# Zeroing the slot buffer: twelve of 79 fills moved from late attention steps to steps 4 and 8

## The chip, the cores and the metric

The kernel runs on one NeuronCore of a Trainium2 chip. The metric is the device time of one execution in microseconds. The core has five engines that work side by side and meet at semaphores: TensorE (PE, with its weight loads shown apart as PEld), VectorE (DVE), ScalarE (ACT), GpSimd (POOL) and SyncE (SP). SP computes nothing; it issues DMAs in the order of its program and waits for semaphores between them. The DMAs themselves run on the core's 16 DMA engines.

## The reference, cut to what matters

One decoder layer in float32 on one sequence of 2048 tokens of width 512.

```python
x = x + attention(layernorm(x), ...)   # q, k, v: projection, short conv, silu; delta rule with state S; rms norm; Wo
x = x + ffn(layernorm(x), ...)

# ffn
cw = combine_weights(xt, gate_w)       # softmax over 16 experts, 2 of 4 groups, top 4 experts, normalised
for e in range(16):
    out = out + cw[:, e:e+1] * (swiglu(xt @ up[e].T) @ down[e].T)
out = out + swiglu(xt @ shared_up.T) @ shared_down.T
```

In the kernel the 2048 tokens form 16 tiles of 128 rows. For the experts the kernel gathers tokens: each of the 2048 x 4 chosen (token, expert) pairs is written as a row of 532 bytes into `slot_rows` in DRAM, a buffer of NQ = 79 slots of 128 rows (64 full tiles and up to 15 tiles that are only partly filled). A row that nobody writes must be zero, so the whole buffer is zeroed before the rows are scattered into it. What is moved here is the zeroing.

## The kernel before, in words

**The attention** (`attention`, first 565 us) is one hand-written schedule. A step `u` runs from -8 to 18, and each step has six slots `s` = 0 to 5. Every engine has its own copy of the same double loop and issues in slot (u, s) what belongs there; the engines are held together by semaphores alone. Step u works on tile u of the delta rule (the hops through the state S on PE, L1081, L1107 and L1147, L1121, L1126), on the projections of later tiles, and on the norm, gate logits and stores of tiles u-1, u-2 and u-3. One step takes some 28 us in the middle of the attention.

**The inverse.** Per tile a triangular matrix (its gram blocks) must be inverted. Four tiles are inverted together on DVE (`inverse`, parts 0 to 8, first instruction L1484). To lay the blocks of four tiles over the lanes, SP stores the gram blocks of each tile to DRAM (`store_gram`, L401, four DMAs) and loads them back turned (`load_lanes`, L408), which waits until the four stores of that tile have landed. For the tiles 12 to 15 this happens in steps 8 to 10: stores and loads of tile 12 and 13 in step 8, the store of tile 14 in step 9 slot 4, `load_lanes(14)` and `store_gram(15)` in step 9 slot 5, `load_lanes(15)` in step 10 slot 0. DVE starts the inverse of these four in step 10 slot 1. On DVE the row sums of the output (L1464), the copy of the gate logits (`lg`, L1478) and the residual Rs (L1448) of that step stand behind it. The four tiles 8 to 11 do the same in steps 4 to 6.

**Weights and the shared expert.** From step 10 on SP also loads the shared expert's weights: the first part of `shared_up` in step 10, its second part in step 12 slot 0 together with two tiles of partial sums (`sq`), and `shared_down` (L441, L442) with the second group of turned activations (`front_region<-x2n_turned`, L447, four DMAs of 256 KB) in step 13 slot 0. PE fits matmuls of the shared expert between the hops, two to a slot (L1204, L1214 for gate and up of the shared units).

**The zero fills.** `zero_rows` (L454 to L457) issues one DMA on SP that fills the next slot of 128 rows from a small tile of zeros:

```python
            def zero_rows():
                if zeroed[0] < NQ:
                    sp.dma_start(rows[zeroed[0]], zeros[:, :].unsqueeze(1).to_broadcast([P, DC, RW // DC])).then_inc(s_zeroed, 16)
                    zeroed[0] += 1
```

It waits for nothing, and nothing waits for it until the end of the attention (`attention_stored`). It is called at the end of a slot, so it stands on SP's queue behind all that the slot issues. Calls beyond the 79th do nothing. Twelve are issued in the opening slots, the others one to a slot from step 0 on, except where the condition at L564 leaves slots out.

**After the attention** come the routing, the scatter of rows into `slot_rows` (GpSimd), the rest of the shared expert and the loop over the 79 slots with the experts' weights, where PE is bound by its matmuls.

Of the kernel before, what the change touches and what calls it, by code (L numbers as in the profile page):

```python
# [201 lines left out]
def attention(nc, es, x_d, wq_d, wk_d, wv_d, wb_d, cq_d, ck_d, cv_d, nw_d, wo_d, gw_d, shu_d, shd_d, region, wsh,  # L202
# [180 lines left out]
    with nc.Block() as block:  # L383

        @block.sync
        def _(sp):
# [67 lines left out]
# [4 lines that stand above are left out]
# [16 lines left out]
            for u in range(FIRST, LAST):  # L474
                even = u % 2 == 0
                for s in range(SLOTS):
# [85 lines left out]
                    if 19 <= opening(u, s) < 28 or 33 <= opening(u, s) < 36:  # L562
                        zero_rows()
                    if u >= 0 and not (u % 4 == 3 and s >= 2) and not (u % 4 == 1 and s >= 4) and not (u % 4 == 2 and s < 1) \  # L564
                            and not (u == 10 and s >= 2) and not (u == 11 and s < 2):
                        zero_rows()
            assert zeroed[0] == NQ
            for par in range(2):
# [1826 lines left out]
```

How the kernel before makes its waits and increments, by code:

```python
def local_routing(dve, link, linked, lg, z, sc, rank, sel, mx, sm, gs, grank, gsel, tri, pa, pb, s_z, s_e, s_sel, lo, n, part):  # L116
# [21 lines left out]
        link(dve.tensor_tensor(pa[:, 0:m * k * k], pa[:, 0:m * k * k], pb[:, 0:m * k * k], ALU.add))  # L138
        linked()
        link(dve.tensor_reduce(out, pa[:, 0:m * k * k].rearrange("p (t e j) -> p t e j", e=k, j=k), AX.X, ALU.add))
    if part == 0:
        linked()
        link(dve.tensor_reduce(mx[:, at], lg[:, at, :], AX.X, ALU.max))
        linked()
        dve.tensor_tensor(z[:, at, :], lg[:, at, :], over(mx[:, at], E), ALU.subtract).then_inc(s_z, 1)
    if part == 1:
        dve.wait_ge(s_e, done + 1)
        link(dve.tensor_reduce(sm[:, at], z[:, at, :], AX.X, ALU.add))
        linked()
        link(dve.reciprocal(sm[:, at], sm[:, at]))
# [22 lines left out]
        if part % 2 == 0:  # L174
            beats(sc[:, four, :], pa, E, ALU.is_gt)
            beats(sc[:, four, :], pb, E, ALU.is_equal)
            linked()
            ties_of_earlier(TPG, E)
        else:
            count(rank[:, four, :], TPG, E)
    if part == 4 + ranks:
        linked()
        dve.tensor_scalar(sel[:, at, :], rank[:, at, :], float(K), None, ALU.is_lt).then_inc(s_sel, 1)
        dve.wait_ge(s_sel, done + 1)
        link(dve.tensor_tensor(sc[:, at, :], sc[:, at, :], sel[:, at, :], ALU.mult))
        linked()
        link(dve.tensor_reduce(sm[:, at], sc[:, at, :], AX.X, ALU.add))
# [8 lines left out]
def least(eng, sem, n):  # L196
    if n > 0:
        eng.wait_ge(sem, n)
```

## Time and profile before

| | |
|---|---|
| median of 3 runs | 1313.39 us (1312.79 to 1316.36) |
| the profiled execution | 1320.15 us |
| its span in the profile | 1318.4 us |
| mean granted clock of TensorE | 0.987 |
| busy: PE / DVE / ACT / POOL | 97% / 66% / 28% / 26% of the span |
| moved by DMA | 171.09 MB, mean 130 GB/s |

Windows count in microseconds from the span's start. The granted clock is a share of full speed: 1.00 is 2.4 GHz, 0.50 is 1.2 GHz, and a number between them is a stretch that had both. The DMA share is the time of the packets as a share of 16 engines; since packets overlap, it can be over 1 where the engines are full. A DMA row on SPq shows how long SP took to issue, not how long the data travelled; for several DMAs in a row it is the time from the first issue to the end of the last.

### The profile page before, as it was taken

How to read it: one execution, taken by the hardware profiler on the slowest of the kernel's cores; microseconds unless marked ns; L12 is line 12 of the kernel's file. 1: busy time of each engine (PE TensorE's matmuls, PEld its weight loads, DVE VectorE, ACT ScalarE, POOL GpSimd, SP SyncE). 2: the span in 40 equal slices, each digit the busy share in tenths (PEclk: the TensorE clock that was granted, in tenths of full speed). 3: DMA queues.
4: the chain of work that ended last, by engine and by line, in shares of the span. 5: the costliest groups of instructions: out<-in, count | busy, mean ns of one | idle time of the engine just before them, and what ended most of it. 6: DMA issues, size and time to landing. Idle time of an engine off the chain costs nothing.

```text
span 1318.4 us, 27847 instructions
## 1 busy us (share of the span) xinstructions
PE 1275.2 (97%) x8725; PEld 795.6 (60%) x8726; DVE 866.4 (66%) x2411; ACT 373.7 (28%) x818; POOL 340.3 (26%) x398
## 2 busy tenths in 40 slices
PE   7979999999999999999999999999999999999997
PEld 6857777877876555443444555555555555555553
DVE  4897698769779226544111677777777777777774
ACT  4754655654553223220000011111111111111111
POOL 1202225323242222115652021222121212122212
PEclk9989999999997999999999999999999999999999
DMA  5434853752653694575457456666666666564420
GB/s 162 86 54 93 135 118 82 163 119 68 131 120 125 156 205 107 130 236 207 182 212 236 111 131 132 138 133 138 136 138 134 132 134 132 131 138 71 74 50 9
DMA packets 208517, 171.09 MB, mean 130 GB/s; under 512 B 71473, under 2 KB 160561, under 8 KB 208433
## 3 DMA queue, kind: packets, MB, share of 16 engines
q1 hardware_dynamic: 135056, 114.16, 34.0%
q0 software_dynamic: 16496, 34.23, 13.3%
q10 hardware_dynamic: 56880, 21.54, 7.8%
q8 instruction: 57, 0.93, 0.3%
q14 instruction: 28, 0.22, 0.1%
HBM read 91.06 MB, written 82.73 MB: 132 GB/s over the span
## 4 chain that ended last, share of the span: by engine, by line
PE 54%; DVE 2%; issue 0%; DMA 0%; POOL 0%; ACT 0%; DVEq 0%; POOLq 0%
PE pD L2300 15%; PE pG L2275 14%; PE pU L2284 14%; PE pG L2232 3%; PE pU L2232 3%; PE pD L2251 3%; PE pU L2226 1%; PE pD L2246 0%; DVE ups L2173 0%; DMA out<-y,ix 0%; DVE w L1873 0%; DVE w L1874 0%; DVE route_keep L1872 0%; POOL out L2065 0%; DVE qf L1885 0%
## 5 line engine op out<-in xcount | busy, mean ns | idle before, releaser
L2173 DVE STREAM_TRANSPOSE ups<-a 32x96 f32<-32x96 f32 (+1 forms) x1248 | 326.0, 261 | 42.4
L2065 POOL DMA_INDIRECT out<-y,ix x79 | 123.0, 1557 | 479.1 <-ACT y L2126 306.7
L2300 PE MATMUL pD<-w,ups 128*128 (+1 forms) x474 | 216.6, 592 | 0.7 <-DVE ups L2173 0.7
L2284 PE MATMUL pU<-w,xsT 128*128 x632 | 199.9, 459 | 0.0
L2275 PE MATMUL pG<-w,xsT 128*128 x632 | 199.9, 458 | 0.0
L2275 PEld LDWEIGHTS pG<-w,xsT 128*128 128x128 f32 x632 | 119.5, 189 | 88.4 <-issue 37.6
L2284 PEld LDWEIGHTS pU<-w,xsT 128*128 128x128 f32 x632 | 120.1, 190 | 66.9
L974 PE MATMUL pProj<-front_region 128*128 128x256 f32 x624 | 153.7, 389 | 2.2 <-ACT front_region L711 1.6
L2300 PEld LDWEIGHTS pD<-w,ups 128*128 128x128 f32 (+1 forms) x474 | 90.0, 190 | 93.2 <-issue 76.8
L974 PEld LDWEIGHTS pProj<-front_region 128*128 128x128 f32 x624 | 112.6, 190 | 19.8 <-ACT front_region L711 2.0
L2126 ACT ACTIVATE y<-pD,wq 128x512 f32<-128x512 f32 x79 | 54.3, 687 | 246.7 <-PE pD L2300 236.9
L2115 ACT ACTIVATE g<-pG 128x352 f32<-128x352 f32 x79 | 36.7, 464 | 260.2 <-DVE xsT L2161 176.6
L1386 DVE SCALAR_TENSOR_TENSOR front_region<-front_region,cw 128x256 f32<-128x256 f32 x216 | 102.3, 515 | 10.5 <-ACT front_region L747 8.0
L2194 DVE TENSOR_TENSOR a<-g,pU 128x352 f32<-128x352 f32 x79 | 41.2, 521 | 89.1 <-PE pU L2284 81.1
L2050 POOL DMA_INDIRECT slot_rows<-xall,pos x64 | 62.8, 981 | 52.4 <-DMA slot_rows<-xall,pos 47.2
L636 POOL TENSOR_TENSOR TT<-TT,ng 128x512 f32<-128x512 f32 x16 | 17.7, 1106 | 223.7 <-ACT TT L789 137.9
L1448 DVE TENSOR_TENSOR Rs<-pC,vh 64x512 f32<-64x512 f32 x32 | 22.0, 688 | 60.2 <-PE pC L1081 59.9
L1164 PE MATMUL pT<-wo,oT 128*128 128x512 f32 x128 | 59.1, 604 | 0.4 <-ACT oT L816 0.4
L2161 DVE STREAM_TRANSPOSE xsT<-xs 128x512 f32<-128x512 f32 x79 | 55.6, 703 | 5.6 <-DMA xs<-slot_rows 4.9
L2251 PE MATMUL pD<-front_region 128*128 128x512 f32 x120 | 53.1, 597 | 0.0
L746 ACT ACTIVATE front_region<-pProj 128x256 f32<-128x256 f32 x78 | 30.1, 385 | 77.5 <-PE pProj L974 75.3
L2232 PE MATMUL pG<-front_region 128*128 128x512 f32 x112 | 50.4, 593 | 0.6 <-PEq L383 0.6
(258 smaller groups left out, 1651.1 us busy)
## 6 DMA issues: line engine op xcount, KB each, us to landing
w<-in_up_T SPq DMA_DIRECT2D x16, 1408.0 KB
slot_rows<-zeros SPq DMA_DIRECT2D x79, 266.0 KB
xs<-slot_rows ACTq DMA_DIRECT2D x316, 64.0 KB
w<-in_down_T SPq DMA_DIRECT2D x16, 512.0 KB
front_region<-in_L_attn_hidden_states SPq DMA_DIRECT2D x16, 256.0 KB, 3.9
x2r<-in_L_attn_hidden_states SPq DMA_DIRECT2D x16, 256.0 KB, 4.5
partial_sums<-x2r SPq DMA_DIRECT2D x16, 256.0 KB, 3.4
x_normed<-x2n SPq DMA_DIRECT2D x16, 256.0 KB, 2.0
```

Of the source, the lines that this page charges most:

```text
L974: mm = pe.matmul(proj_bank(g), w3[:, w, k, cols(i % DC, P)], xnT[p % 2][:, k, :], start=(k == 0), stop=(k == DC - 1))
L1164: mm = pe.matmul(pT1[:, 0, :], oT[:, k, :], wo[:, k, :], start=(k == 0), stop=(k == DC - 1))
L1386: ins = dve.scalar_tensor_tensor(out=acc[(g + h) % len(acc)], in0=raw[:, at, j:j + PW], scalar=cw[:, at, j:j + 1], in1=acc[(g + h) % len(a ...
L2050: pool.indirect_dma_start(out=xs_d[:, :], out_offset=bass.IndirectOffsetOnAxis(ap=pos[:, i, j:j + 1], axis=0), in_=xall[:, i, :], in_offse ...
L2065: pool.indirect_dma_start(out=flat, out_offset=bass.IndirectOffsetOnAxis(ap=ix[1 - par][:, 0:1], axis=0), in_=y[1 - par][:, :], in_offset= ...
L2161: dve.transpose(xsT[par][:, :, :].rearrange("p k (a i) -> p a k i", a=BLOCKS), xs[par][:, :].rearrange("p (a k j) -> p a k j", a=BLOCKS, k ...
L2173: dve.transpose(aT[par][B * to:B * to + B, 0:n, rows], a[rows, 0:len(IC) * P].rearrange("p (c n) -> p c n", c=len(IC))[:, 0:n, B * to:B * ...
L2232: mm = pe.matmul(p[:, :], wsh["up"][:, k, at:at + P], xg[gr % 2][:, k, :], start=(k == 0), stop=(k == DC - 1))
L2251: mm = pe.matmul(sdown(j)[:, :], sa[:, c, P * i:P * i + P], wsh["down"][:, c, :], start=False, stop=(c == UNITS - 1))
L2275: mm = pe.matmul(pG[0][:, 0:I], xsT[par][:, k, :], w[:, bass.ds(slot, 1), 2 * I * k:2 * I * k + I], start=(k == 0), stop=(k == DC - 1))
L2284: mm = pe.matmul(pU[0][:, 0:I], xsT[par][:, k, :], w[:, bass.ds(slot, 1), 2 * I * k + I:2 * I * (k + 1)], start=(k == 0), stop=(k == DC - 1))
L2300: mm = pe.matmul((pYlast if end(q) else pYq)[:, :], aT[1 - par][0:m, c, :], down[0:m, :, UPW + D * c:UPW + D * (c + 1)], start=(c == 0), s ...
```

## The change

The condition under which a slot of the steps from 0 on issues a zero fill leaves out steps 12 and 13 now, and in steps 4 and 8 every slot issues a second one.

```diff
                     if u >= 0 and not (u % 4 == 3 and s >= 2) and not (u % 4 == 1 and s >= 4) and not (u % 4 == 2 and s < 1) \
-                            and not (u == 10 and s >= 2) and not (u == 11 and s < 2):
+                            and not (u == 10 and s >= 2) and not (u == 11 and s < 2) and u not in (12, 13):
+                        zero_rows()
+                    if u in (4, 8):
                         zero_rows()
```

The fills by step, before and now: step 4: 6 and 12; step 8: 6 and 12; step 12: 6 and 0; step 13: 4 and 0; step 16: 5 and 3 (the count of 79 is reached sooner); all other steps as before.

SP in step 8, before: the stores of tile 12 (L401), its lane load (L408), the stores and the lane load of tile 13, with fills (L456) between.

```order
177 L401 DMA gram_blocks<-NP 32x8x32 x3
178 L456 DMA slot_rows<-zeros 512x1x133 x2
179 L408 DMA front_region<-gram_blocks 32x1024 [waits inverse_done,gram_stored0]
...
184 L456 DMA slot_rows<-zeros 512x1x133
185 L401 DMA gram_blocks<-NP 32x8x32 [waits gram_scaled]
186 L401 DMA gram_blocks<-NP 32x8x32 x3
187 L456 DMA slot_rows<-zeros 512x1x133
188 L408 DMA front_region<-gram_blocks 32x1024 [waits inverse_done,gram_stored1]
189 L456 DMA slot_rows<-zeros 512x1x133
```

The same place of SP's queue now:

```order
177 L401 DMA gram_blocks<-NP 32x8x32 x3
178 L456 DMA slot_rows<-zeros 512x1x133 x4
179 L408 DMA front_region<-gram_blocks 32x1024 [waits inverse_done,gram_stored0]
...
184 L456 DMA slot_rows<-zeros 512x1x133 x2
185 L401 DMA gram_blocks<-NP 32x8x32 [waits gram_scaled]
186 L401 DMA gram_blocks<-NP 32x8x32 x3
187 L456 DMA slot_rows<-zeros 512x1x133 x2
188 L408 DMA front_region<-gram_blocks 32x1024 [waits inverse_done,gram_stored1]
189 L456 DMA slot_rows<-zeros 512x1x133 x2
```

Every fill of the step is doubled, ahead of the next tile's stores and of the loads that wait for them; step 4 has the same picture with tiles 8 and 9.

SP in steps 12 and 13, before, from the second load of partial sums (L452) to the last fill of step 13's first two slots:

```order
242 L452 DMA sq<-partial_sums 128x512 [waits x2_stored1]
243 L456 DMA slot_rows<-zeros 512x1x133 x2
244 L520 DMA x_normed<-x2n 128x512 [waits x2n_ready]
245 L522 DMA x2n_turned<-x2g 128x512 [waits x2nT_ready]
246 L456 DMA slot_rows<-zeros 512x1x133
247 L526 DMA x2r<-in_L_attn_hidden_states 128x512 [waits x2_stored0,x2n_ready]
248 L456 DMA slot_rows<-zeros 512x1x133 x3
249 L488 DMA partial_sums<-x2r 128x512 [waits x2_ready]
250 L441 DMA front_region<-in_shared_down_T 64x512 x2
251 L442 DMA front_region<-in_shared_down_T 128x5x512
253 L447 DMA front_region<-x2n_turned 128x4x128 x3
254 L456 DMA slot_rows<-zeros 512x1x133 x2
```

The same place now:

```order
242 L452 DMA sq<-partial_sums 128x512 [waits x2_stored1]
243 L520 DMA x_normed<-x2n 128x512 [waits x2n_ready]
244 L522 DMA x2n_turned<-x2g 128x512 [waits x2nT_ready]
245 L526 DMA x2r<-in_L_attn_hidden_states 128x512 [waits x2_stored0,x2n_ready]
246 L488 DMA partial_sums<-x2r 128x512 [waits x2_ready]
247 L441 DMA front_region<-in_shared_down_T 64x512 x2
248 L442 DMA front_region<-in_shared_down_T 128x5x512
250 L447 DMA front_region<-x2n_turned 128x4x128 x3
```

No fill stands ahead of or behind the weight loads any more; the order of everything else is as it was. No other engine's order changes.

## Rows read from the trace of the kernel before

**Rows 1.** The page: busy time by engine; instruction queue (packets, MB); the zero fills.

```profile
PE 1275.2 (97%) x8725; PEld 795.6 (60%) x8726; DVE 866.4 (66%) x2411; ACT 373.7 (28%) x818; POOL 340.3 (26%) x398
...
q8 instruction: 57, 0.93, 0.3%
...
slot_rows<-zeros SPq DMA_DIRECT2D x79, 266.0 KB
```

**Rows 2.** Windows: length, busy us of PE, PEld, DVE, ACT, POOL; clock, DMA share, GB/s.

```profile
457.00:464.00 7.00, 7.00 (x117) 4.32 (x113) 2.29 (x5) 2.35 (x5) 2.34 (x6) 1.00 1.15 214
464.00:470.00 6.00, 4.30 (x70) 2.69 (x69) 0.77 (x2) 1.78 (x3) 3.10 (x4) 1.00 1.24 127
470.00:475.00 5.00, 5.00 (x41) 3.02 (x40) 0.00 (x0) 0.98 (x2) 0.00 (x0) 0.66 1.04 200
```

**Rows 3.** Timeline of PE's weight loads, step 13: start, us, instruction, idle before.

```profile
466.66 0.19 PEld L1214 LDWEIGHTS pT<-front_region 128*128 128x128 f32 x1 [0.24 <-issue]
469.37 0.19 PEld L1214 LDWEIGHTS pT<-front_region 128*128 128x128 f32 x1 [2.52 <-issue]
```

**Rows 4.** Timeline of SP's queue, steps 12 and 13.

```profile
458.19 4.39 SPq L456 DMA_DIRECT2D slot_rows<-zeros  x3
...
465.48 0.64 SPq L442 DMA_DIRECT2D front_region<-in_shared_down_T  x1
466.16 10.54 SPq L447 DMA_DIRECT2D front_region<-x2n_turned  x4
```

**Rows 5.** Timeline of SP's queue, steps 9 and 10: gram stores and lane loads.

```profile
376.86 1.94 SPq L401 DMA_DIRECT2D gram_blocks<-NP  x4
382.19 0.31 SPq L408 DMA_DIRECT2D front_region<-gram_blocks  x1
383.38 2.40 SPq L401 DMA_DIRECT2D gram_blocks<-NP  x4
...
386.99 0.31 SPq L408 DMA_DIRECT2D front_region<-gram_blocks  x1
```

**Rows 6.** DMA issues in 386.9 to 387.2 us: KB each, us to landing.

```profile
front_region<-gram_blocks SPq DMA_DIRECT2D x1, 128.0 KB, 2.3
```

**Rows 7.** Timeline of DVE, step 10.

```profile
389.30 0.17 DVE L1484 COPY route_keep<-front_region 128x4 f32<-128x4 f32 x1
...
392.61 0.17 DVE L1478 COPY lg<-pT 128x16 f32<-128x16 f32 x1 [1.16 <-PE pT L1178]
...
396.75 0.69 DVE L1448 TENSOR_TENSOR Rs<-pC,vh 64x512 f32<-64x512 f32 x1
```

**Rows 8.** Timeline of PE, step 10.

```profile
393.80 0.66 PE L936 MATMUL pT<-ident,x2n 128*128 128x128 f32 x4
...
397.59 0.24 PE L1107 MATMUL pC<-Rs,TT 64*64 64x64 f32 x1 [0.16 <-DVE Rs L1448]
```

**Rows 9.** Timelines of SP's queue and of DVE, step 6: the same for tiles 8 to 11.

```profile
275.79 0.34 SPq L408 DMA_DIRECT2D front_region<-gram_blocks  x1
...
284.18 0.17 DVE L1484 COPY route_keep<-front_region 128x4 f32<-128x4 f32 x1
```

**Rows 10.** Windows of steps 8 and 9, and one of dense zero fills (step 0).

```profile
349.00:361.00 12.00, 12.00 (x145) 8.56 (x142) 7.68 (x17) 6.05 (x16) 0.00 (x0) 1.00 1.09 202
361.00:362.50 1.50, 1.50 (x29) 1.22 (x23) 0.04 (x1) 1.50 (x5) 0.00 (x0) 1.00 0.17 21
370.00:374.50 4.50, 4.50 (x93) 3.94 (x91) 3.98 (x10) 3.13 (x7) 4.31 (x3) 1.00 0.18 65
142.00:149.00 7.00, 6.81 (x144) 5.58 (x142) 5.00 (x10) 5.54 (x14) 6.24 (x11) 1.00 1.22 143
```

**Rows 11.** Windows at half clock: in the opening, and in steps 10 and 11.

```profile
95.40:102.20 6.80, 6.42 (x48) 5.15 (x49) 6.70 (x11) 2.55 (x7) 2.52 (x5) 0.50 0.01 2
406.00:419.60 13.60, 12.60 (x148) 8.92 (x143) 13.34 (x19) 3.64 (x7) 6.62 (x9) 0.50 0.19 62
```

## Prediction

> **What bounds the kernel now.** I read the page first. TensorE (PE) is busy 97% of the span [rows 1], so only two things can move the end: a stretch in which PE stands, and a stretch in which its clock is halved. The change moves DMAs alone, so I looked, with the views of windows and of timelines, for places where a DMA stands behind such a stretch. There are two in the attention.
>
> **Place A, step 13, around 468 us.** Between 464 and 470 us PE is busy 4.30 of 6.00 us, while the DMA engines are more than full (share 1.24) and yet move only 127 GB/s; in 457 to 464 they moved 214 [rows 2]. The weight-load timeline shows the hole: in the middle of one tile (pT by L1214, where nothing is waited for) the next load comes 2.52 us late, "issue" being all that the profile can say [rows 3]. Behind it the granted clock is 0.66 in 470 to 475 [rows 2], a mixture of 2.4 and 1.2 GHz. SP's own timeline shows the crowd: three zero blocks take 4.39 us to issue, and the four loads of x2n_turned 10.54 us, against some 0.5 us for one where the queue is free (four in 1.94 us [rows 5]).
>
> **Place B, step 10, 389.3 us.** The last load of the gram lanes (L408, tile 15) is issued at 386.99 [rows 5] and lands 2.3 us later [rows 6], at 389.29. VectorE (DVE) begins the inverse of the last block (L1484), which waits for it, at 389.30 [rows 7]. That load has no slack: by how much it comes later, by so much DVE stands. DVE matters there: it runs nearly without a gap up to Rs at 396.75 [rows 7], and PE waits 0.16 us for that Rs at 397.59 [rows 8].
>
> **The change, part by part.** In the code 79 zero blocks stay 79. Steps 12 and 13 lose six and four, step 16 its last two (all 79 are out before); steps 4 and 8 gain six each. Each is one SP DMA of 266 KB [rows 1], without a wait of its own. Nothing on PE, DVE, ScalarE or GpSimd changes.
>
> *Removed in steps 12 and 13.* The six blocks of step 12 stand ahead of the shared down weights and the x2n_turned loads [rows 4]. What remains in the queue moves in long rows and finds its place before 466 us. I take it that the hole goes, since it fell in the stretch of lowest rate: 6.00 - 4.30 = 1.70 us of PE, and the clock's share, (1 - 0.66) x 5 = 1.7 us, together **-3.4 us**. Bounds: 0 if something else made the hole; -4.2 if all 2.52 us of the late weight load counts beside the clock. PE is busy all of 457 to 464 and of 470 to 475 [rows 2], so what is won there is not lost to another wait.
>
> By the Trainium skill ("Runtime: NRT & Kernel Launch", Instruction fetch mechanics) an engine's instructions come in 16 KiB blocks by a DMA queue, mostly hidden. The instruction queue of the page has 57 packets with 0.93 MB [rows 1], 16 KB each, which agrees. By that rule the hole is a block of instructions that came late through full DMA engines; the sum would be the same -3.4.
>
> *Added in step 4.* One block more in each slot. The next inverse starts at 284.18 behind other DVE work, while its last lane load is issued at 275.79 [rows 9]; with 2.3 us to land, as in [rows 6], that leaves 6.1 us. There are free stretches too. I count 0 here; if that cover is gone, the price is that of place B.
>
> *Added in step 8.* One block costs the DMA engines 1.9 us where they carry zero blocks back to back (272 KB at 143 GB/s, 142 to 149 us) and 1.35 us at the mixed rate of step 8 (202 GB/s) [rows 10]. The share is already 1.09 in 349 to 361, so six more are a queue of 6 x 1.9 = 11.4 us, or 8.1. What is free after it is 0.83 x 1.5 us at 361 and 0.82 x 4.5 us at 370 [rows 10], together 4.9 us. So the gram store of tile 14 (issued 376.86 [rows 5]) lands 6.5 us later, or 3.2. From there on all is serial on SP: lane load 14 at 382.19, store of 15 at 383.38, lane load 15 at 386.99 [rows 5]. The store at 383.38 had waited 0.9 us for its own input (382.19 + 0.31 to 383.38), which is used up first: lane load 15 comes 5.6 us late, or 2.3. On DVE 1.2 us of that is taken by the wait for PE ahead of lg at 392.61 [rows 7], since that input is there by then. PE stands 4.4 us, or 1.1: the x2n transposes at 393.80 need the logits behind the inverse, and Rs comes last [rows 8]. I take **+4.4 us**, since the queue will be as in 142 to 149. Bounds: 0 if the packets of a short store get through beside the zeros, +5.6 if DVE's slack does not help.
>
> By the Trainium skill ("DMA: Bandwidth & Descriptors", Queues, rings and completion order) descriptors are consumed in ring order on each DMA engine, and all DMAs of SP share its rings. That speaks against this change: a gram store cannot pass the zeros. By it the sum has the +4.4; a fair share for each DMA would leave out nearly all of it. The 5.3 us from the store's issue at 376.86 to the lane load at 382.19, which waits for it, go with ring order.
>
> *The clock behind that stall.* The stop of PE at place A was followed by 1.7 us lost to the clock [rows 2]; in the opening the clock was 0.50 for 6.8 us [rows 11], 3.4 us of work. But PE is at 0.50 anyway from 406 to 419.6 [rows 11], and DVE is nearly full there (13.34 of 13.60 us), which hides part. Bounds 0 and +3.4; I take **+1.7**, the smaller of the two measured, for the overlap.
>
> *SP itself.* Twelve more issues of some 0.5 us in steps 4 and 8 lie beside SP's waits; they come within the queue counted above. Step 16's two fewer: 0.
>
> Sum: -3.4 + 0 + 4.4 + 1.7 = **+2.7 us**. The profiled execution took 1320.15 us (span 1318.4), 6.8 above the median of 1313.39; on the median the sum gives 1316.1, on a profile of the change about 1322.9.
>
> **The rivals.**
> 1. *The stall at B without the gain at A, slower.* The hole is not of the zeros' making, or is not in the unprofiled runs, which are 6.8 us shorter. Then +4.4 and 1.7 to 3.4 of clock: +6.1 to +7.8, 1319.5 to 1321.2. It decides once A gives under 2.2 us (2.7 + 3.4 - 3.9). For it: "issue" names nobody. Against: the rate of 127 GB/s just there.
> 2. *The hole moves, slower.* In steps 4 and 8 the DMA engines are now as full as at 464; a hole like that of [rows 3] costs 1.7 and 1.7 again: +6.1, 1319.5. Against: in 142 to 149, at share 1.22, PE is busy 6.81 of 7 us [rows 10]. The skill's rule on instruction blocks (Instruction fetch mechanics) bears on this.
> 3. *The delay is absorbed, faster.* The lane loads come in time or PE has other work, and A gives all: -3.4 to -4.2, 1309.2 to 1310. For it: a single store is small. Against: lane load 15 lands 10 ns before it is used.
> 4. *Nothing moves in effect.* The order on SP does change, so this can only be by both places being nothing: 0, part of the forecast's band.
>
> **How the numbers follow.** A measurement of this kernel tells about 0.3% from no change, 3.9 us: 1309.5 to 1317.3. Forecast with rival 4: 0.46, its own range 1312 to 1319, about a quarter of it over 1317.3. Rival 1: 0.20. Rival 2: 0.12. Rival 3: 0.22, two thirds of it over the faster bound. Faster 0.15; slower 0.20 + 0.12 + 0.11 = 0.43; same 0.42. The range reaches from rival 3 to rival 1: 1309 to 1322.
>
> **What would show it.** Right: in the windows of the changed kernel PE is full in 464 to 475 at clock 1.00; the DMA share is over 1 from about 350 to 378; lane load 15 is issued at about 392.6 instead of 386.99, L1484 (two lines further down now) starts about 5.6 us later, and PE shows a wait of some 4 us for DVE near 394 to 402. Wrong: L1484 starts within 1 us of 389.3, or the late weight load in the shared up tiles of step 13 is still there, or a new one stands in steps 4 to 9. If the last inverse waits and the end is still earlier by over 3.9 us, the account of PE's cover is wrong.

## The result and the profile after

The changed kernel is slower: 1320.76 us median of 7 runs (1318.87 to 1323.33) against 1316.32 us for the kernel before on the same chips (7 runs, 1312.79 to 1319.61); ratio 1.0041, 95% interval 1.0023 to 1.0058, or +5.4 us (3.0 to 7.6). (The ratios here are those on record; they are not exactly the quotients of the medians, which differ by 4.4 us here.) The forecast was 1316.1 us, +2.7 us, from a gain of 3.4 us at place A and a loss of 6.1 us at place B. The time lies inside the range, and the direction is the one with the largest chance, but it came out as rival 1 had it: all of the loss, none of the gain. In microseconds both need care: the forecast was added to a median of 1313.39 us (3 runs), and the same kernel's median in the comparison is 2.9 us higher, so of the 4.7 us between 1320.76 and the forecast more than half is the base. As a difference, the +2.7 us lies just under the interval, and the lower end of rival 1's +6.1 to +7.8 lies inside it. The profiled execution took 1323.33 us, as the forecast for a profile said (1322.9), and that agreement is itself half an accident, as the experiments show.

The page of the changed kernel: span, PE's busy time, the clock in 40 slices, the fills.

```profile
span 1321.6 us, 27847 instructions
...
PE 1274.9 (96%) x8725; PEld 797.2 (60%) x8726; DVE 866.9 (66%) x2411; ACT 373.3 (28%) x818; POOL 339.4 (26%) x398
...
PEclk9989999999996999999999999999999999999999
...
slot_rows<-zeros SPq DMA_DIRECT2D x79, 266.0 KB, 7.6
```

PE does the same work (1275.2 us in [rows 1]) in a longer span; the clock's digit in slice 13 (396 to 430 us) is 6, where the kernel before has a 7. There the waits view (390 to 404 us: engine, line, what it waited for, us in total, times, longest) has:

```profile
DVE route_keep L1486 <- DMA front_region<-gram_blocks: 7.4, 1, 7.4
ACT x2g L831 <- PE pT L938: 5.9, 1, 5.9
PEld pT L938 <- issue: 5.3, 1, 5.3
PE pT L938 <- DVE lg L1480: 5.2, 1, 5.2
```

The chain of place B can be read from the bottom up: the x2n transposes (L938, two lines down from L936) wait for the logits, these come behind the inverse on DVE (L1486, before L1484), and the inverse waits 7.4 us for the last load of the gram lanes. The timelines of DVE and PE, with the wait ahead of each in brackets:

```profile
396.38 0.17 DVE L1486 COPY route_keep<-front_region 128x4 f32<-128x4 f32 x1 [7.40 <-DMA front_region<-gram_blocks]
```
```profile
398.87 1.08 PE L938 MATMUL pT<-ident,x2n 128*128 128x128 f32 x4 [5.18 <-DVE lg L1480]
...
403.70 0.24 PE L1109 MATMUL pC<-Rs,TT 64*64 64x64 f32 x1 [0.16 <-DVE Rs L1450]
```

L1486 starts at 396.38 where [rows 7] had 389.30, 7.1 us later. SP's queue tells why:

```profile
376.58 0.63 SPq L456 DMA_DIRECT2D slot_rows<-zeros  x1
380.02 0.33 SPq L526 DMA_DIRECT2D x2r<-in_L_attn_hidden_states  x1
380.39 0.54 SPq L456 DMA_DIRECT2D slot_rows<-zeros  x1
380.98 3.70 SPq L401 DMA_DIRECT2D gram_blocks<-NP  x4
389.15 0.31 SPq L408 DMA_DIRECT2D front_region<-gram_blocks  x1
389.51 2.73 SPq L401 DMA_DIRECT2D gram_blocks<-NP  x4
392.28 0.45 SPq L488 DMA_DIRECT2D partial_sums<-x2r  x1
394.21 0.31 SPq L408 DMA_DIRECT2D front_region<-gram_blocks  x1
```

Lane load 14 goes out at 389.15 instead of 382.19 and lane load 15 at 394.21 instead of 386.99 [rows 5]: 7.0 and 7.2 us late. Of these 7.0 us, 4.1 come already ahead of the gram store (issued at 380.98, before at 376.86): the x2r load in front of it waits until a store of partial sums (step 8's) has landed behind the fills, 2.7 us in the waits of SP's queue (370 to 396 us), where the kernel before has no such wait:

```profile
SPq L199 <- DMA partial_sums<-x2r: 2.7, 1, 2.7
```

The loads themselves still take 2 to 3 us to land, so it is the queue ahead, not the load, that is long.

The windows of the stretch and of place A (columns as in [rows 2]):

```profile
349.00:361.00 12.00, 12.00 (x144) 8.53 (x143) 7.50 (x17) 6.04 (x16) 0.00 (x0) 1.00 1.16 188
382.00:395.90 13.90, 11.28 (x269) 9.75 (x260) 3.68 (x7) 6.14 (x14) 2.25 (x5) 1.00 0.58 127
395.90:402.70 6.80, 3.64 (x27) 3.15 (x28) 5.88 (x18) 0.60 (x1) 3.15 (x4) 0.50 0.47 122
413.00:426.70 13.70, 12.06 (x152) 8.67 (x146) 13.47 (x18) 3.48 (x7) 5.92 (x9) 0.50 0.08 30
464.00:470.00 6.00, 6.00 (x104) 3.83 (x102) 1.74 (x4) 2.35 (x5) 2.29 (x5) 1.00 0.85 269
470.00:475.00 5.00, 5.00 (x85) 3.15 (x85) 1.15 (x3) 1.77 (x3) 3.14 (x4) 1.00 0.90 265
```

From 395.9 us, while PE is still standing (393.7 to 398.9 us), the granted clock is 0.50 (1.2 GHz) for 6.8 us; the stretch at half clock of [rows 11] is still there behind it, now from 413.0 us. At place A PE is full in 464 to 475 us at clock 1.00, without a hole.

Step 4 held, but more narrowly than reckoned. SP's queue, the landing of that load (in 278.2 to 278.5 us: KB, us to landing), and DVE:

```profile
278.27 0.37 SPq L408 DMA_DIRECT2D front_region<-gram_blocks  x1
```
```profile
front_region<-gram_blocks SPq DMA_DIRECT2D x1, 128.0 KB, 5.2
```
```profile
284.02 0.17 DVE L1486 COPY route_keep<-front_region 128x4 f32<-128x4 f32 x1
```

The load goes out 2.5 us later than in [rows 9] and takes 5.2 us instead of the 2.3 I lent it from [rows 6]; it lands at 283.5, half a microsecond before its use.

**The same matmuls, stretch by stretch.** Every trace holds all 8725 matmuls of the program, and their order is the same. So I counted the time between the starts of matmuls 4800 and 5500 (392.8 and 450.4 us in the profile of before, around place B), 5700 and 5900 (465.0 and 486.6, around place A) and 1500 and 4000 (163.6 and 340.4, around step 4). All the kernels below are in one table; "late" is the issue of lane load 15 against 386.99, both counted from the start of matmul 4000; "PE wait" is PE's longest wait ahead of the transposes of step 10 (for the logits in after, e1, e4 and e6, and for vh in the others, where it is 0.7 to 1.1 us and belongs to the kernel before too); the ratio is that of the timed runs with its interval.

```
kernel            1500-4000  4800-5500  5700-5900  late   PE wait   ratio (95%)
before              176.8      57.6       21.5      0      0.7 us   1
before, again       176.6      57.9       17.9      0.1    1.1
before, third       176.6      57.9       17.9      0.0    1.1
after               176.6      64.3       17.9      7.4    5.2      1.0041 (1.0023-1.0058)
e1_step8_only       176.6      64.1       17.9      7.7    5.5      1.0050 (1.0031-1.0069)
e2_step4_for12      176.6      57.0       17.9      0.3    0.7      1.0004 (0.9988-1.0019)
e3_step6            176.6      57.2       17.9     -0.2    1.1      1.0004 (0.9987-1.0022)
e4_act_ring         176.8      60.9       18.0      4.4    2.5      1.0008 (0.9991-1.0024)
e5_three_in_8       176.6      57.2       17.9     -0.2    1.1      0.9990 (0.9975-1.0005)
e6_triple_8         176.8      72.5       18.3     16.3   14.1      1.0100 (1.0068-1.0132)
e7_triple_4         184.3      57.2       17.9      0.0    1.1      1.0066 (1.0044-1.0087)
e8_double_12_13     176.6      56.9       18.5      0.0    0.7      1.0051 (1.0033-1.0070)
f3_step9_free       176.6      57.9       17.9      0.3    0.9      0.9996 (0.9980-1.0011)
```

Where PE does not wait for the logits, the 56.9 to 57.9 us around place B go with the stretch at half clock that begins between 404 and 412 us: it is 13.7 us long in the three profiles of before and in f3 (57.6 us and more), and 10.2 us in e2, e3, e5, e7 and e8 (57.2 and less).

The two profiles first compared differ by +6.7 us at place B and -3.6 us at place A, and by 0.3 us or less elsewhere: the forecast's two places, at nearly the forecast's sizes. But the 21.5 us at place A stand in that one execution of before alone.

### The profile page after: what moved, and what is told of

Its sections match the earlier page's. It is cut to its first block, busy times and chain, and to the rows that moved or that the text cites. A ratio compares the mean times of both kernels' runs of the same rounds, so it can differ in the third digit from the quotient of the medians.

```text
span 1321.6 us, 27847 instructions
## 1 busy us (share of the span) xinstructions
PE 1274.9 (96%) x8725; PEld 797.2 (60%) x8726; DVE 866.9 (66%) x2411; ACT 373.3 (28%) x818; POOL 339.4 (26%) x398
## 4 chain that ended last, share of the span: by engine, by line
PE 54%; DVE 2%; issue 0%; DMA 0%; POOL 0%; ACT 0%; DVEq 0%; POOLq 0%
PE pD L2302 15%; PE pG L2277 14%; PE pU L2286 14%; PE pG L2234 3%; PE pU L2234 3%; PE pD L2253 3%; PE pU L2228 1%; PE pD L2248 0%; DVE ups L2175 0%; DMA out<-y,ix 0%; DVE w L1875 0%; DVE w L1876 0%; DVE route_keep L1874 0%; POOL out L2067 0%; DVE qf L1887 0%
```

## The experiments

**The theory and its rivals.** The queue theory: fills hold up what SP issues behind them, by their own DMA time less what is free in between, and the time is lost where the last late transfer is used without slack. Rival 1 to it (for place B): it is not the queue's order but full DMA engines, so that the same bytes from another queue cost the same. Rival 2: the loss is something else and the late lane load only accompanies it. For place A there were two theories as well: the fills of steps 12 and 13 make the hole, or they don't.

### Step 8 alone, with the fills of steps 12 and 13 (e1_step8_only)

```diff
+                    if u == 8:
+                        zero_rows()
```

> Only step 8 is doubled; steps 12 and 13 keep their fills, step 4 its six (the count ends earlier, in steps 15 and 16). Place B alone (the last lane load of the inverse late): lane load 15 issued near 394 us, TensorE idle some 5.2 us before 399 and 6.8 us of half clock behind it, as in the changed kernel; the hole with the late weight load in step 13 stays. The theory that B alone makes the loss expects 7 to 9 us over before in the profile and in the timed runs (ratio 1.005 to 1.007). The rival, that dense fills anywhere cost time (step 4 as much as step 8), expects half of the change's loss, 1.002, and the same in the run with step 4 alone.

Measured 1321.92 us (11 runs) against 1314.69 (34 runs), 1.005 (1.0031 to 1.0069). As large a loss as the change's comes from these six fills alone. Waits (388 to 400 us) and windows:

```profile
DVE route_keep L1486 <- DMA front_region<-gram_blocks: 7.8, 1, 7.8
...
PE pT L938 <- DVE lg L1480: 5.5, 1, 5.5
```
```profile
394.60:401.40 6.80, 5.29 (x40) 4.36 (x42) 6.00 (x15) 1.20 (x2) 3.15 (x4) 0.50 0.41 115
...
464.00:470.00 6.00, 6.00 (x118) 4.16 (x117) 2.89 (x6) 1.36 (x3) 3.37 (x7) 1.00 1.20 223
470.00:475.00 5.00, 5.00 (x59) 2.81 (x57) 0.00 (x0) 1.40 (x3) 0.33 (x1) 1.00 1.18 119
```

The last two lines are the surprise. The six fills of step 12 are still ahead of the weight loads here, the DMA share is 1.20, the rate falls to 119 GB/s (before: 127 at the hole), and PE is full at clock 1.00. Crowded DMA engines do not by themselves make the hole.

### Steps 12 and 13 emptied, without step 8 (e2_step4_for12, e3_step6)

e2 takes the fills out of step 12 only and doubles step 4; e3 takes both steps' out and puts them into step 4 and five slots of step 6.

```diff
-                            and not (u == 10 and s >= 2) and not (u == 11 and s < 2):
+                            and not (u == 10 and s >= 2) and not (u == 11 and s < 2) and u != 12:
+                        zero_rows()
+                    if u == 4:
                         zero_rows()
```

> The six fills of step 12 go to step 4; steps 8 and 13 are as before. The theory of place B expects no wait of VectorE for the lanes in step 10 (last inverse begins within 1 us of 389.3) and nothing lost in steps 4 to 6; if the six fills of step 12 alone made the hole of step 13, it goes: 0 to 3.4 us faster than before. The rival of dense fills anywhere expects 2 to 3 us slower.

```diff
+                            and not (u == 10 and s >= 2) and not (u == 11 and s < 2) and u not in (12, 13):
+                        zero_rows()
+                    if u in (4, 6) and not (u == 6 and s < 1):
                         zero_rows()
```

> As the change, but the fills of step 8 go to step 6 (slots 1 to 5, one more at the end), where after the lane load of tile 11 nothing is on SP's queue that an engine waits for soon. The theory expects place A's gain alone: no TensorE hole in step 13, clock 1.00 there, last inverse near 389.3: 3 to 4 us faster than before in the profile, ratio about 0.997 in timed runs if their hole is there too. The rival, that the loss of the change is the density of fills, expects the changed kernel's time, 1.004.

Measured 1315.60 us (12 runs) and 1315.71 us (12 runs) against the same 1314.69: 1.0004 (0.9988 to 1.0019) and 1.0004 (0.9987 to 1.0022). Neither shows a loss, so step 4's doubling is free, and place B stays as it was (57.0 and 57.2 us). But neither gains the 0.26% that 3.4 us are; both intervals leave that out. The expected 0.997 of e3 failed, and with it the gain at place A: had the timed runs of the kernel before had the hole as a rule, both would show it.

### The kernel before, twice more (f1_before_again, f2_before_third)

No edit; one profile each, to see whether the hole belongs to the kernel or to one execution.

> The kernel before, unchanged, profiled once more. If the hole in step 13 (1.70 us of TensorE without a releaser, half clock behind it) belongs to the kernel, it is there again near 466 to 470 us. If it came by chance, there is none, as in the runs with six, ten or twenty fills in steps 12 and 13, and the half clock of steps 10 and 11 may have another length.

> The kernel before, unchanged, a third look, with the same two answers: a hole near 466 to 470 us, or none.

1314.74 and 1316.79 us. Place A in the first (windows, then the weight loads that answer to [rows 3]):

```profile
457.00:464.00 7.00, 7.00 (x125) 4.31 (x120) 2.12 (x4) 1.75 (x5) 4.04 (x8) 1.00 1.17 227
464.00:470.00 6.00, 6.00 (x70) 3.43 (x68) 0.77 (x2) 2.55 (x5) 1.40 (x2) 1.00 1.12 143
470.00:475.00 5.00, 5.00 (x52) 2.91 (x49) 1.38 (x2) 1.78 (x3) 0.00 (x0) 1.00 1.06 331
```
```profile
464.80 0.19 PEld L1214 LDWEIGHTS pT<-front_region 128*128 128x128 f32 x1 [0.24 <-issue]
465.23 0.19 PEld L1214 LDWEIGHTS pT<-front_region 128*128 128x128 f32 x1 [0.24 <-issue]
```

The same instruction of the same kernel with as full a queue (in the 6 us up to the last matmul ahead of the hole the DMA share was 1.20 at 202 GB/s; up to the same matmul it is 1.21 at 208 here, 1.20 at 178 in the third, 1.21 at 222 in e1): 0.24 us of issue where [rows 3] had 2.52, and no clock loss behind it. The third profile of before shows the same (17.9 us). One in three profiles of before had the hole, and none of the ten of other kernels here. That execution also was the slow end of its kind: 1320.15 us beside medians of 1314.7 to 1316.3. These two profiles come from one chip and those of e1 to e8 from two others, and the chip of the first is not on record, so a property of its chip is not excluded. The third has a dip of its own, 3.4 us at half clock from 602.2 us (+1.9 us in the stretch around it), so such strays come elsewhere too.

One thing was different in the first profile next to the hole: the instruction queue. Its rows in the DMA view (packets, MB, share of 16 engines) have, for the last packet ahead of the hole in before (465 to 468 us), for the last one ahead of the same matmul in before again (460 to 463 us), and for one in e5 (275 to 279 us):

```profile
q8 instruction: 1, 0.02, 4.4%
```
```profile
q8 instruction: 1, 0.02, 2.3%
```
```profile
q8 instruction: 1, 0.02, 4.1%
```

4.4% of 16 engines over 3 us is one packet of 2.1 us, from 465.4 to 467.5 us, the longest of the 57 in that trace, and PE stops at 467.7. In the second profile it took 1.1 us. That fits a block of instructions that came late. But PE went on only 1.8 us after this packet had ended, and e5 has a longer one (2.6 us) with PE busy all through. So it is a trace of the cause at most, and not shown to be it.

### The doubled fills of step 12 and 13 (e8_double_12_13)

The rest of the fills, brought forward into steps 12 and 13, should make the hole come always, if they make it.

```diff
+                    if u in (12, 13):
+                        zero_rows()
```

> Steps 12 and 13 are doubled (12 and 8 fills), the count ends in step 14; all else as before. If the fills beside the shared weights make the hole in TensorE's instruction stream (the late weight load without a releaser), it must be there now, larger (3 us or more) or several times, with half clock behind it, and the time 4 us or more over before (1.003 or more). If the hole came by chance and the fills cost nothing there, the time is before's (0.999 to 1.001).

Measured 1321.97 us (10 runs) against 1314.71 (25 runs), 1.0051 (1.0033 to 1.007). Slower, but not by the hole: the weight loads of step 13 come without the 2.5 us, and 5700 to 5900 takes 18.5 us. The loss is around step 14: 5.9 us more than in the others between matmuls 5900 and 6100, and 2.1 us more up to 6500. Windows, waits (488 to 504 us) and landings (issues in 490 to 491 us):

```profile
464.00:470.00 6.00, 5.67 (x60) 3.17 (x60) 0.77 (x2) 2.74 (x5) 1.59 (x2) 1.00 1.19 207
...
499.00:505.80 6.80, 4.46 (x10) 1.96 (x10) 2.66 (x9) 4.71 (x7) 0.00 (x0) 0.50 1.21 200
```
```profile
ACT x2g L831 <- DMA x2n_turned<-x2g: 7.6, 1, 7.6
...
PE pT L938 <- ACT x2g L831: 5.9, 1, 5.9
```
```profile
x2n_turned<-x2g SPq DMA_DIRECT2D x1, 256.0 KB, 9.9
```

ScalarE may not write the next x2g before the store of the last one has read it; that store takes 9.9 us to land behind the fills, and PE waits for ScalarE. Neither expectation had this: the loss is there, but by a path that neither named. It is the queue theory at a third place, with another buffer, and again there are 6.8 us at half clock, from 499.0 us, inside PE's wait.

### The same bytes from ScalarE's queue (e4_act_ring)

Steps 12 and 13 empty, step 4 doubled, and the second fill of each slot of step 8 issued by ScalarE instead of SP (SP's own count ends at 73 in return).

```diff
+            def zero_rows_act(q):
+                act.dma_start(rows[q], zeros[:, :].unsqueeze(1).to_broadcast([P, DC, RW // DC])).then_inc(s_zeroed, 16)
...
+                    if u == 8:
+                        zero_rows_act(NQ - SLOTS + s)
```

> As the change, but the second fill of each slot of step 8 is issued on ScalarE's queue. If the gram stores are late because they stand behind the fills in SP's own rings, they pass now: lane load 15 near 387 to 390, TensorE's stall under 2 us, time below before (ratio about 0.998). If they are late because the DMA engines and DRAM are full, lane load 15 is still 4 to 7 us late and the time is the change's, ratio 1.003 to 1.005.

Measured 1317.21 us (12 runs), 1.0008 (0.9991 to 1.0024). Waits (388 to 400 us) and SP's queue:

```profile
DVE route_keep L1493 <- DMA front_region<-gram_blocks: 4.7, 1, 4.7
...
PE pT L945 <- DVE lg L1487: 2.5, 1, 2.5
```
```profile
389.68 0.31 SPq L408 DMA_DIRECT2D front_region<-gram_blocks  x1
```

Neither expectation came true: the lane load is 4.4 us late instead of 7.4, and PE waits 2.5 us instead of 5.2. The stretch around place B is 3.0 us longer than in the later profiles of before; the timed runs can't tell that from nothing. So taking the fills out of SP's queue does not remove the delay, and the bytes count whoever issues them: the fills' place in SP's queue is not the whole cause. How much of the 3.0 us by which the load is less late belongs to the queue's order stays open, because the edit changed a second thing. ScalarE does not stand behind SP's waits and issues its fills earlier, the first and the last of the six at

```profile
335.80 0.71 ACTq L850 DMA_DIRECT2D slot_rows<-zeros  x1
...
360.10 0.54 ACTq L850 DMA_DIRECT2D slot_rows<-zeros  x1
```

while in the changed kernel SP issues the fills of that step from 346.4 us on. Fills that are out earlier have had more free time behind them when the gram store comes.

### Three instead of six in step 8 (e5_three_in_8)

```diff
+                    if u == 4 or (u == 8 and s < 3) or (u == 6 and 1 <= s < 4):
+                        zero_rows()
```

(with the fills of steps 12 and 13 out, as in e3)

> As the change, but only slots 0 to 2 of step 8 are doubled (three fills), the other three go to slots 1 to 3 of step 6. The queue theory: 3 x 1.9 = 5.7 us of added queue against 4.9 us free and 0.9 us of slack on SP: lane load 15 within 1 us of before, no stall over 1.5 us in step 10, time as before (0.999 to 1.001). The rival, that any fill added to step 8 delays in proportion, expects half of the change's loss: stall 2.5 us, ratio 1.002 to 1.003.

Measured 1314.48 us (10 runs) against 1314.71, 0.999 (0.9975 to 1.0005). SP's queue:

```profile
385.84 0.31 SPq L408 DMA_DIRECT2D front_region<-gram_blocks  x1
```

With the openings' shift that is 0.2 us earlier than before: three fills, 5.7 us of DMA time by the forecast's price, fit into the free time behind step 8 and the slack on SP, six don't.

### Two more in each slot of step 8 (e6_triple_8)

```diff
+                    if u == 8:
+                        zero_rows()
+                    if u == 8:
                         zero_rows()
```

(with the fills of steps 12 and 13 out)

> The twelve fills all go to step 8 (three in a slot), step 4 has its six. The queue theory: six fills more than the change at 1.9 us each, none of it free: lane load 15 another 11 us later (about 18 us after before's), TensorE idle about 16 us in step 10 instead of 5.2, and the time 1.3% over before (17 us, plus or minus 3). A rival, that TensorE finds other work or that the cost levels off, expects under 1.008.

Measured 1329.33 us (5 runs) against 1314.71, 1.01 (1.0068 to 1.0132). Waits (388 to 410 us):

```profile
DVE route_keep L1488 <- DMA front_region<-gram_blocks: 16.3, 1, 16.3
...
PE pT L940 <- DVE lg L1482: 14.1, 1, 14.1
```

Six more fills than after make the lane load 8.9 us later (16.3 against 7.4), 1.5 us each where the forecast had 1.9, and PE's stall 8.9 us longer: once the slack is gone, each microsecond of queue is one of stall. So the stall (16 us) and the time (1.3%) were forecast too high. A loss that only kept company with the late load would not scale so in the profile; the timed runs alone, with an interval from 1.0068, would not exclude the rival's 1.008.

### Two more in each slot of step 4 (e7_triple_4)

```diff
+                    if u == 4:
+                        zero_rows()
+                    if u == 4:
                         zero_rows()
```

(with the fills of steps 12 and 13 out)

> The twelve fills all go to step 4 (18 there), step 8 has its six. In the changed kernel lane load 11 landed at 283.5 us, 0.7 us before the inverse of tiles 8 to 11 used it. Six more fills there are 11.4 us: TensorE should stall about 10 us in step 6 and the time be 0.8% (8 to 13 us) over before. If steps other than 8 are harmless by their place, there is no stall and the ratio is 1.000.

Measured 1323.97 us (9 runs) against 1314.71, 1.0066 (1.0044 to 1.0087). Waits (284 to 304 us) and window:

```profile
DVE route_keep L1488 <- DMA front_region<-gram_blocks: 8.1, 1, 8.1
...
PE pC L1111 <- DVE Rs L1452: 6.8, 1, 6.8
```
```profile
291.90:302.10 10.20, 6.19 (x37) 3.66 (x38) 9.82 (x22) 3.61 (x8) 0.36 (x1) 0.50 0.54 76
```

The mechanism of place B at step 4, 7.7 us in its stretch: six fills used up the slack there, six more are paid for. It reaches PE through Rs, not through the logits. The expected stall of about 10 us was too high; the time (+0.7%) is in the expected band.

### Step 8 doubled, step 9 free (f3_step9_free)

If it is the queue in front of the gram store, fills behind step 8's have to count as well as its own.

```diff
-                            and not (u == 10 and s >= 2) and not (u == 11 and s < 2):
+                            and not (u == 10 and s >= 2) and not (u == 11 and s < 2) and u not in (9, 12, 13):
+                        zero_rows()
+                    if u in (4, 8) or (u == 6 and 1 <= s < 5):
                         zero_rows()
```

> As the change, with steps 4 and 8 doubled, but the four fills of step 9 go to step 6. The queue theory: the store of tile 14 now has 4 x 1.9 = 7.6 us less ahead of it, so lane load 15 is back within 1 us of before's place, TensorE's stall in step 10 is under 1.5 us and the time is before's (0.999 to 1.001), although step 8 is as full as in the change. If a doubled step 8 is harmful as such, the time is the change's, 1.004.

Measured 1315.88 us (10 runs) against 1316.22 (13 runs), 0.9996 (0.998 to 1.0011). SP's queue:

```profile
387.14 0.31 SPq L408 DMA_DIRECT2D front_region<-gram_blocks  x1
```

0.3 us late, and no wait of PE beyond the 0.9 us for vh. Step 8 is doubled as in the change, and it costs nothing: what matters is how many fills are outstanding when the gram store of tile 14 comes, not which step they are in.

Of all these, none beats the kernel before by more than can be told; the nearest, e5 and f3, are level with it.

## Why the prediction was right and wrong

**Place A, -3.4 us: wrong, and it is the step that failed.** I wrote "I take it that the hole goes, since it fell in the stretch of lowest rate". The changed kernel has no hole, but neither has the kernel before in 2 of its 3 profiles, and if its timed runs had had it as a rule, e2 and e3 would have been faster. As full a queue without a hole (143 GB/s at 1.12 in the second profile of before, 119 at 1.18 in e1) and the 1.0004 of e2 and e3 put the term at 0. The bound of 0 "if something else made the hole" and rival 1's words on the unprofiled runs named this case; with a single profile, and a releaser that read "issue", it deserved more than 0.20. What the hole was stays open. By the Trainium skill ("Runtime: NRT & Kernel Launch", Instruction fetch mechanics) an engine fetches its instructions in blocks of 16 KiB while it executes the ones before, at a cost that is mostly hidden. A block that came late would leave a gap like this one, with nothing waited for, and the 2.1 us packet of the instruction queue just ahead of it fits; but four profiles with DMA engines as full and no hole (before again, before third, e1 and e8) speak against the fills as a sufficient cause, and e5's packet of 2.6 us against a long packet alone.

**Place B, +4.4 us of stall: right.** Every link is there: store, lane load, inverse, logits, transposes. The size came out partly by luck, since the links were off in both directions. The lane load came 7.2 us late (forecast 5.6): the queue came to 7.0 us at lane load 14 (6.5), SP's 0.9 us of slack was used up as reckoned (the store of tile 15 went out 6.1 us late), but that store then held lane load 15 for 1.1 us more than before. Also, more than half of the 7.0 us came ahead of the gram store, through the wait of the x2r load, which I had not seen. DVE's wait for PE ahead of lg took its 1.2 us: L1486 is 7.1 us later, the copy of the logits 5.9 us (398.55 against 392.61 in [rows 7]). PE came to the transposes 1.0 us after the copy of the logits had ended in the kernel before, and 0.15 us after it now, so it had some 0.9 us of its own in hand; it stood 5.2 us, from which goes the wait of 0.7 us for vh that before had in the same place and that I had left out: net 4.5. The short store did not slip through (bound 0), and DVE's slack did help (bound 5.6). With the 4.9 us of free time as I had estimated it, the first six fills cost 2.0 us each (1.9); for the next six, e6 shows 1.5.

By the Trainium skill ("DMA: Bandwidth & Descriptors", Queues, rings and completion order) a DMA engine takes the descriptors of a ring in order, and SP and ScalarE have rings of their own on the same 16 engines. If the order in SP's ring were all, e4 would have taken the whole delay away. It left 4.4 of 7.4 us, so the order is not all; whether it has a part, e4 can't say, since its fills also went out earlier.

**The clock, +1.7 us: the size is right, the cause is shown only in part.** The stretch around place B is 6.7 us longer (6.4 against the second profile of before); less the net stall, 2.2 us are left. PE's busy time in that stretch grew by 1.4 us (54.8 in all three profiles of before, 56.1 after), and that is what the clock can be charged with; the rest is small waits of 0.4 to 1.1 us behind the stall. For e1, e4 and e6 the same subtraction (stretch against 57.9, stall less 1.1) gives 1.7, 1.6 and 1.6 for stalls of 2.5 to 14.1 us, but PE's busy time is 55.5, 54.9 and 54.9: in e4 and e6 the later stretch at half clock is shorter (6.8 us instead of 13.7), and nearly all that is left over is waits. So a stall cost 1.6 to 2.2 us beyond itself each time, and the clock is the larger part of it only in the changed kernel.

**Step 4, 0: right, for a thinner reason.** I gave it 6.1 us of slack; half a microsecond was left. Both the later issue and the slower landing were missing, and e7 shows that what lies behind this is as dear as place B.

**The sum.** With A at 0 the forecast's own terms give 4.4 + 1.7 = +6.1 us, and the measured stretches +6.7 (6.4 against the other two profiles of before); the timed runs have +5.4 (3.0 to 7.6). The +3.2 us between the two first spans (1318.4 and 1321.6) would have seemed to confirm +2.7; they are +6.7, -3.6 and noise. Rival 2, a new hole in steps 4 and 8, is in none of the profiles. Rival 3, the delay absorbed, holds for three fills (e5) and for six when step 9 is free (f3).

## What to carry to other kernels

A DMA that nobody waits for still has a price: the time that it takes from the DMA engines (1.4 to 2 us for one of these) less what is free before the next transfer whose landing someone uses at once. So reckon slack as landing to use, with the landing time of a crowded queue, for each transfer behind it: lane loads, stores that free a buffer, loads that wait for a store. And before a gap without a releaser is made a term of a sum, take a second profile of the same kernel, and compare the time between the same matmuls in both.

## What was unexpected of the hardware

- A weight load can come 2.5 us late, with PE standing for 1.7 us and "issue" as the only cause, in one execution, and after 0.24 us in the next of the same kernel; 1.5 us after PE had gone on, the clock fell to half for 3.4 us. Together 3.6 us, more than many edits are worth.
- Each stall of PE of 2.4 us or more inside the attention's steps in these profiles was met by a stretch at half clock: 6.8 us (after, e1, e4, e8), 10.2 (e7), 17.1 (e6, in which PE stood for much of it). It began while PE stood. At place B the stretch lost 1.6 to 2.2 us beyond the stall whatever the stall's length, by the clock or by small waits.
- The stretch at half clock that begins near 404 to 413 us differs between executions whose order is the same up to there: 13.7 us in all three profiles of before, 10.2 in e8, which differs from before only from step 12 on.
- The opening, from the first matmul to matmul 1500, takes 157.0 to 161.3 us from one profile to another, with no edit in it. Spans of single profiles differ by that already; the unedited stretches behind it agree to 0.3 us.
- Six fills on ScalarE's queue instead of SP's, and out earlier, still delay a load on SP's queue by 4.4 us (7.4 with all on SP's queue).
